# Attention heads of an mLSTM and mixture-of-experts layer taken in pairs, their score products alternating between the two halves of the array's rows

## What is computed

```
xn   = layernorm(x)                       # queries
ig,fg= gates from [xn, ctx, ctx]          # 8 + 8 rows per token
cs   = cumsum(log_sigmoid(fg))
logD[s,t] = cs[s] - cs[t] + ig[t]   for t <= s, else -inf
Dmat = exp(logD - max_t logD)
C    = (xn_h @ ctx_h.T / 8) * Dmat        # 256 x 256, lower triangle, per head
h    = C / (max(|sum C|, exp(-max logD)) + 1e-6) @ ctx_h
x    = x + tanh(g0) * layernorm(h) * ln_scale
```

## Time and profile before

| | |
|---|---|
| runs | 1310.32, 1306.76, 1304.9 us; median 1306.76 |
| span of the profiled execution | 1302.3 us, first to last instruction; its own total time is not listed apart |
| PE busy | 1098.4 us, 84% |
| PEld | 910.9 us, 70% |
| DVE | 827.1 us, 64% |
| ACT | 371.4 us, 29% |
| POOL | 491.8 us, 38% |

### The profile page before, as it was taken

The page is one execution under the profiler, slowest core; times in us unless marked ns, Lnnn a source line. Parts: engine busy times, 40 slices in busy tenths (PEclk is TensorE's granted clock), DMA queues, the critical chain, the costliest instruction groups (busy, mean ns, idle before and its releaser), DMA issues.

```text
span 1302.3 us, 24291 instructions
## 1 busy us (share of the span) xinstructions
PE 1098.4 (84%) x6611; PEld 910.9 (70%) x6612; DVE 827.1 (64%) x2212; ACT 371.4 (29%) x820; POOL 491.8 (38%) x368
## 2 busy tenths in 40 slices
PE   2289999999999999999999765999999999999000
PEld 1167888878788887788788664788888888887000
DVE  3756878888788788788877644544444444444455
ACT  1133233424333333343333102223233232232000
POOL 3600222222222222222212335356656566700775
PEclk9666999999999999999999778999999999999555
DMA  5000001110111011001000244555464645321787
GB/s 205 32 33 33 33 34 66 57 42 32 65 57 41 33 65 65 17 32 49 33 1 34 82 172 156 175 181 176 158 205 149 209 151 187 128 98 64 239 283 260
DMA packets 57869, 134.53 MB, mean 103 GB/s; under 512 B 7088, under 2 KB 7088, under 8 KB 57808
## 3 DMA queue, kind: packets, MB, share of 16 engines
q0 software_dynamic: 17472, 59.78, 14.0%
q1 hardware_dynamic: 26128, 48.51, 11.2%
q10 hardware_dynamic: 14208, 25.57, 5.5%
HBM read 83.23 MB, written 50.59 MB: 103 GB/s over the span
## 4 chain that ended last, share of the span: by engine, by line
PE 72%; DVE 12%; issue 7%; DMA 5%; ACT 2%; POOL 0%; DVEq 0%; ACTq 0%; POOLq 0%
PE bank L1137 18%; PE bank L1001 10%; PE bank L1155 9%; PE bank L1012 7%; PE bank L937 5%; PE bank L913 5%; DMA area<-routed_y,y_at 4%; PE bank L879 3%; PE bank L1125 3%; PE bank L942 2%; PE bank L954 2%; PE bank L939 2%; PE bank L955 2%; PE bank L957 2%; PE bank L1146 1%
## 5 line engine op out<-in xcount | busy, mean ns | idle before, releaser
L1137 PE MATMUL bank<-w_ring,x2nT 128*128 x960 | 246.0, 405 | 8.6 <-DVE w_ring L1597 8.6
L1137 PEld LDWEIGHTS bank<-w_ring,x2nT 128*128 128x128 f32 x960 | 175.3, 189 | 48.9 <-issue 10.0
L1001 PE MATMUL bank<-x2nT,w_ring 128*128 128x256 f32 x1536 | 200.2, 288 | 7.8 <-DVE sh_act L1434 7.8
L1001 PEld LDWEIGHTS bank<-x2nT,w_ring 128*128 128x128 f32 x1536 | 190.2, 194 | 9.2 <-DVE sh_act L1434 5.4
L501 POOL DMA_INDIRECT routed_x<-x2n,slot_u x64 | 67.5, 1054 | 192.9 <-DVE slot_u L1424 178.3
L1288 DVE SCALAR_TENSOR_TENSOR area<-bank,area 128x384 f32<-128x384 f32 x128 | 71.4, 557 | 96.7 <-ACT area L712 61.4
L1155 PE MATMUL bank<-w_ring,sh_actT 128*128 x480 | 125.2, 396 | 2.1 <-DVE sh_actT L1616 2.1
L1603 DVE SCALAR_TENSOR_TENSOR ctxT<-ctxT,bank 128x256 f32<-128x256 f32 x80 | 33.7, 421 | 142.7 <-ACT ctxT L826 142.7
L710 ACT ACTIVATE area<-bank,key_log 128x256 f32<-128x256 f32 x128 | 60.7, 474 | 212.1 <-PE bank L944 176.2
L522 POOL TENSOR_TENSOR sh_actT<-sh_act,sh_actT 128x256 fp32r<-128x256 f32 x64 | 54.5, 852 | 167.9 <-ACT sh_actT L727 167.8
L618 POOL TENSOR_TENSOR w_ring<-area,one 128x3072 fp32r<-128x3072 f32 x14 | 74.3, 5304 | 114.4 <-PE bank L1155 114.4
(11 more groups left out here) (203 smaller groups left out, 2059.0 us busy)
## 6 DMA issues: line engine op xcount, KB each, us to landing
x2n<-routed_x SPq DMA_DIRECT2D x80, 256.0 KB, 2.8
routed_y<-cs_in ACTq DMA_DIRECT2D x80, 256.0 KB, 2.1
base_out<-in_x_dram SPq DMA_DIRECT2D x16, 512.0 KB, 4.4
cs_in<-in_ctx_dram SPq DMA_DIRECT2D x16, 512.0 KB, 3.7
area<-n_L_ffn_expert_gate_dram POOLq DMA_DIRECT2D x16, 512.0 KB, 4.1
area<-in_L_ffn_expert_up_dram POOLq DMA_DIRECT2D x16, 512.0 KB, 4.9
area<-n_L_ffn_expert_down_dram POOLq DMA_DIRECT2D x16, 512.0 KB, 6.9
out_dram<-area SPq DMA_DIRECT2D x32, 256.0 KB, 4.2
```

The costliest lines, as they stand in the source:

```text
L1001: last = mm(GU[m][:, at:at + S], w[:, w_part, c, m * P:(m + 1) * P], x2nT[:, x_part, c, :], start=(c + p == 0), stop=(c == DC - 1 and p == 2))
L1137: last = mm(bank[2 + t.par][:, :], xtT[:, x_part, t.par, c * P:(c + 1) * P], w_gu[:, bass.ds(slot, 1), w_part, c, :].rearrange("p a i -> p ...
```

## The change

The eight heads are taken two at a time. PE's `head` becomes `pair(b, q)`, which makes the scores of heads `2q` and `2q + 1` with the products of the two alternating, then spreads both maxima. `c_made` and `decay_made` of both heads of the pair before must be in. The number and size of all products stay. The `step` lists of ACT, PE and DVE are put in an order that follows; POOL's and SP's stay as they are.

```diff
-            def head(b, h):
-                k = h % 2
-                rows = slice(DH * (h % 2), DH * (h % 2) + DH)
-                c = h // 2
+            def pair(b, q):
                 pe.wait_ge(xnT_made.sem, xnT_made.upto(b.n))
                 pe.wait_ge(ctxT_made.sem, ctxT_made.upto(b.n))
                 pe.wait_ge(row_step.sem, row_step.upto(b.n))
-                pe.wait_ge(c_made.sem, c_made.upto(b.n, h - 1))
-                pe.wait_ge(decay_made.sem, decay_made.upto(b.n, h - 1))
-                mm(QK[k][:, 0:S], ctxT[rows, b.par, c, 0:P], xnT[rows, b.par, c, 0:S],
-                   start=True, stop=True)
-                mm(QK[k][:, S:TRI], ctxT[rows, b.par, c, P:S], xnT[rows, b.par, c, P:S],
-                   start=True, stop=True).then_inc(qk_made.sem, 1)
-                for at, n in ((0, S), (S, P)):
-                    mm(MB[k][:, at:at + n], head_sel[0:96, h, :], max_parts[0:96, b.par, S - n:S],
-                       start=True, stop=False)
-                    last = mm(MB[k][:, at:at + P], identb[:, :], mask_b[:, :], start=False, stop=True)
-                last.then_inc(max_spread.sem, 1)
+                pe.wait_ge(c_made.sem, c_made.upto(b.n, 2 * q))
+                pe.wait_ge(decay_made.sem, decay_made.upto(b.n, 2 * q))
+                for at, frm, n in ((0, 0, S), (S, P, P)):
+                    for k in range(2):
+                        half = slice(DH * k, DH * (k + 1))
+                        last = mm(QK[k][:, at:at + n], ctxT[half, b.par, q, frm:frm + P], xnT[half, b.par, q, S - n:S],
+                                  start=True, stop=True)
+                        if at:
+                            last.then_inc(qk_made.sem, 1)
+                for k in range(2):
+                    for at, n in ((0, S), (S, P)):
+                        mm(MB[k][:, at:at + n], head_sel[0:96, 2 * q + k, :], max_parts[0:96, b.par, S - n:S],
+                           start=True, stop=False)
+                        last = mm(MB[k][:, at:at + P], identb[:, :], mask_b[:, :], start=False, stop=True)
+                    last.then_inc(max_spread.sem, 1)
```

The rest of the diff moves calls within the three `step` lists. The lists of a full step, before (-) and after (+), with the calls in one line:

```
- ACT head 0, keep(H,1), shared(H,2), head 1, turn_ctx 0, keep(H,2), shared(H,3), head 2, turn_ctx 1,
      keep(H,3), head 3, turn_x 0, head 4, turn_x 1, top(H), head 5, turn(G,0), head 6, turn(G,1),
      head 7, log_gates(F), shared(G,0), keep(G,0), shared(G,1), columns(F)
+ ACT head 0, 1, keep(H,1), shared(H,2), turn_ctx 0, head 2, 3, keep(H,2), shared(H,3), turn_ctx 1,
      keep(H,3), head 4, 5, turn_x 0, turn_x 1, top(H), head 6, 7, turn(G,0), log_gates(F), turn(G,1),
      shared(G,0), keep(G,0), shared(G,1), columns(F)

- PE  head 0, shared(H,2), head 1, pv 0, turn_ctx 0, shared(H,3), head 2, pv 1, turn_ctx 1,
      shared_down(H,0), head 3, turn_x 0, pv 2, head 4, turn_x 1, pv 3, shared_down(H,1), gates_pe(F),
      head 5, turn(G,0), pv 4, head 6, turn(G,1), rank(H), pv 5, head 7, router(G), shared(G,0),
      logits(G), pv 6, shared(G,1), columns(F), pv 7
+ PE  pair 0, shared(H,2), pv 0, pv 1, turn_ctx 0, pair 1, shared(H,3), pv 2, pv 3, turn_ctx 1, pair 2,
      shared_down(H,0), turn_x 0, pv 4, pv 5, turn_x 1, pair 3, shared_down(H,1), gates_pe(F), pv 6,
      pv 7, turn(G,0), rank(H), turn(G,1), router(G), shared(G,0), logits(G), shared(G,1), columns(F)

- DVE head 0, h_stats(G), shared(H,2), head 1, center(G), stats(N), shared(H,3), head 2,
      norm_front(F,0), x2_add(G), out_pair 0, shared_down(H,0), head 3, norm_front(F,1), x2_stats(G),
      head 4, out_pair 1, post_norm(G), top(H), shared_down(H,1), head 5, turn(G,0), read_gates(F),
      head 6, turn(G,1), rank(H), head 7, out_pair 2, router(G), rows(F), shared(G,0), keep_logits(G),
      shared(G,1), columns(F), out_pair 3
+ DVE head 0, 1, h_stats(G), shared(H,2), center(G), x2_add(G), out_pair 0, head 2, 3, stats(N),
      shared(H,3), x2_stats(G), out_pair 1, norm_front(F,0), head 4, 5, post_norm(G),
      shared_down(H,0), norm_front(F,1), out_pair 2, top(H), head 6, 7, shared_down(H,1),
      read_gates(F), turn(G,0), rank(H), out_pair 3, turn(G,1), router(G), rows(F), shared(G,0),
      keep_logits(G), shared(G,1), columns(F)
```

More of the change, by code:

```diff
@@ L739, in step @@
                     head(A, 0)
+                    head(A, 1)
                 if rest:
@@ L766, in step @@
                 if attend:
-                    head(A, 5)
+                    head(A, 6)
+                    head(A, 7)
                 if route:
                     turn(G, 0)
-                if attend:
-                    head(A, 6)
+                if front:
+                    log_gates(F)
                 if route:
                     turn(G, 1)
[L774 to L777, removed]
                 if route:
@@ L1024, in step @@
                 if attend:
-                    head(A, 0)
+                    pair(A, 0)
                 if rest:
@@ L1057, in step @@
                 if attend:
-                    head(A, 5)
+                    pv(A, 6)
+                    pv(A, 7)
                 if route:
                     turn(G, 0, front)
-                if attend:
-                    pv(A, 4)
-                    head(A, 6)
+                if rest and route:
+                    rank(H, front, attend)
                 if route:
                     turn(G, 1, front)
-                if rest and route:
-                    rank(H, front, attend)
-                if attend:
-                    pv(A, 5)
-                    head(A, 7)
-                if route:
                     router(G, front)
@@ L1479, in step @@
                     shared(H, 3)
-                if attend:
-                    head(A, 2)
-                if front:
-                    norm_front(F, 0)
-                if route:
-                    x2_add(G)
-                if attend:
-                    out_pair(A, 0)
-                if rest:
-                    shared_down(H, 0)
-                if attend:
-                    head(A, 3)
-                if front:
-                    norm_front(F, 1)
                 if route:
@@ L1496, in step @@
                 if attend:
+                    out_pair(A, 1)
+                if front:
+                    norm_front(F, 0)
+                if attend:
                     head(A, 4)
-                    out_pair(A, 1)
+                    head(A, 5)
                 if route:
                     post_norm(G)
+                if rest:
+                    shared_down(H, 0)
+                if front:
+                    norm_front(F, 1)
+                if attend:
+                    out_pair(A, 2)
                 if rest and route:
                     top(H)
+                if attend:
+                    head(A, 6)
+                    head(A, 7)
                 if rest:
                     shared_down(H, 1)
-                if attend:
-                    head(A, 5)
+                if front:
+                    read_gates(F)
                 if route:
                     turn(G, 0)
-                if front:
-                    read_gates(F)
-                if attend:
-                    head(A, 6)
-                if route:
-                    turn(G, 1)
                 if rest and route:
@@ L1517, in step @@
                 if attend:
-                    head(A, 7)
-                    out_pair(A, 2)
+                    out_pair(A, 3)
                 if route:
+                    turn(G, 1)
                     router(G)
```

47 lines of the change are left out of this document (22 added, 25 removed).

## The result

The changed kernel took 1339.25 us (median of 4 runs, 1337.45 to 1341.46) against 1308.54 for the kernel before on the same chip: a ratio of 1.0239 with a 95% interval of 1.0210 to 1.0268. It is 2.4% slower; forecast were 1357 us and a range of 1318 to 1382. The profiled span is 1335.9 us, 33.6 more than before.

What follows compares the result with a forecast made beforehand. PE was taken to bound, with DVE's late results in program order deciding. Thirteen steps of waits (27 us) and clock (23 us) add 50 us to 1306.8, giving 1357 us; range 1318 to 1382.

Steps and rivals of the forecast that it cites:

- waits, but a clock that holds: Rival: same waits, but idle stretches too short to lower the clock; 1334 us, chance 0.30.
- Score products: PE's scores and spreading for two heads: different row groups run concurrently; a pair was counted at 1.8 us.
- Front half: Start of the first pair to xn's second turn: PE ready at 19.5 us, xn at 21.1; PE waits 1.6 us.
- After the branch: The step following DVE's loop branch, every second one, has 1.4 us more of waiting.
- turn(G,1): Second turn of x2n on PE: only rank lies between the turns, so PE waits 1.5 us for DVE.
- router: PE's router waits 2.3 us for DVE's remainder of turn(G,1), held to 36.2 us by DVE's and ACT's queues alike.
- Tail: From router to next pair: router 1.51, two shared blocks 5.9, small turns with waits 0.7 us; next pair at 44.3.
- A full step's waits: Waits in each of steps 2 to 14: 2.1 us more on average, 13 x 2.1 = 27 us.
- The ends: Steps 0, 1 and 15, which lack some parts: put at nothing, 3 us either way.
- Clock: Clock falls just ahead of the router in most steps, returns within router and shared(G,0): 1.8 us a step, 23 in all.
- PE goes on to bound: Rival: both waits, 1.6 and 3.8 us, mostly wrong, so a step gets shorter; 1275 us, chance of faster 0.10.

Runs made afterwards that it cites:

- e4: Changed kernel plus 9 unneeded products ahead of turn(G,1) and 15 ahead of the router, in steps that have all parts; 1319.62 us, ratio 1.0107 to the kernel before.
- e5: Changed kernel with a pair's score products not alternating: all four passes of the even head, then four of the odd; 1339.79 us, ratio 1.0232.
- e9: e6 with both heads of a pair reading rows 0 to 63, so the odd heads' own scores are left out; 1311.34 us, ratio 1.0013.
- e1: Changed kernel with log_gates(F) put behind turn(G,1) again on ACT; 1336.0 us, ratio 1.0250 to the kernel before.
- e2: Changed kernel with out_pair(A,3) put behind turn(G,1) on DVE; 1338.06 us, ratio 1.0256 to the kernel before.
- e6: Changed kernel with PE's turn(G,0) behind the fourth pair, turn(G,1) behind shared_down(H,1), both ahead of the gates, ACT and DVE following; 1285.45 us, ratio 0.9817.
- e10: e6 with DVE's `top` cut in two, one-hots and weights moved behind turn(G,1); 1277.64 us, ratio 0.9754 to the kernel before.
- e3: Changed kernel with both log_gates (ACT) and out_pair(A,3) (DVE) put behind turn(G,1); 1335.24 us, ratio 1.0228 to the kernel before.
- e7: Changed kernel with DVE's norm_front(F,0) and norm_front(F,1) put ahead of x2_stats, post_norm and shared_down(H,0) as inputs allow; 1339.06 us, ratio 1.0231.
- e11: e10 with e7's order on DVE (norm_front(F,0) ahead of out_pair 1, x2_stats behind heads 4 and 5); 1302.89 us, ratio 0.9950.
- e12: e10 with each pair's PE work head by head, scores and spread products of the even head, then the odd; 1316.27 us, ratio 1.0064.
- e8: Changed kernel with the reorderings of e6 and e7 together; 1331.23 us, ratio 1.0173 to the kernel before.

## Why the prediction was right, and where its sizes were off

Slower was right, and by the mechanism forecast: waits of PE for DVE around the two turns of x2n, and a clock that falls because of them. The sum was too high by 19 us: 50 us forecast, 31 (2.4%) measured. By its time alone the result lies in the range of the rival "waits, but a clock that holds"; the granted clock in the windows and e4 exclude that rival. The waits and the clock were both put too high, and the first and last steps, which were put at nothing, gave time back. Of the 19 us some 7 are the clock's, 5 those of the ends and 4 those of the full steps' waits, by the traces; the rest lies between traces and medians.

**Score products: 1.8 us a pair, measured 1.41.** The first score product starts 0.86 us before the first spread product, and the next block 1.41 us after it. The forecast let neighbouring passes overlap only where they lie side by side in the order of issue, five slots. They fall into four, each the size of one head's pass, though each product's two passes were issued together; so a pair's scores cost what one head's do (0.86 against 0.85). The rule of the Trainium skill, "TensorE: Matmul & The Clock Gate", Part 3, that products in different row groups run concurrently, is borne out by e5 and e9. The starts lay 6 to 7 ns apart, and 14 in e5, not the some 4 of the forecast's rule.

**Front half: 1.6 us, measured 2.08.** The waits are 0.75, 0.48 and 0.85 us, 0.5 more, as PE's own work up to there was 0.5 shorter than forecast: what PE gained, it waited. xn's turn starts 21.1 us into the step (413.09 to 434.16), as forecast. Here the forecast's statement that the waits swallow most of the scores' price was right.

**After the branch: 1.4 us more, measured 0.9.** Laps alternate between 45.7 and 46.6 us (before: 42.2 and 43.6 to 43.7).

**turn(G,1): 1.5 us, measured 1.36; router: 2.3, measured 2.29.** That both ACT's logarithm and DVE's rank and out_pair hold it, and that undoing one alone would not help, e1 and e2 show; they end within 0.02 us of each other.

**Tail: 8.1 us, measured 9.95** (449.07 to 459.02), of which the clock is 1.5: 0.4 more than forecast, in short waits ahead of the next pair.

**A full step's waits: 2.1 us, and 27 in all; measured 1.8 and 24.** From the first router to the 14th, thirteen steps, e4 takes 23.6 us more than the kernel before.

**The ends: nothing, 3 us either way; measured -5.** From the 14th router on DVE has less to do (30 us of work in the next step, where a full one has 34 to 35), and the shorter pairs show as a gain: the next two steps are 3.0 and 2.7 us shorter in e4 than before, against 0.6 us lost up to the first router. In the changed kernel 4.1 us are gained at the end and 0.8 at the start. Besides the five slots above, this is where a step of the forecast failed, and not only a size. With them e4's trace is 18.5 us longer up to the experts; by the medians 14 are left.

**Clock: 1.8 us a step and 23 in all; measured 1.2 and 16 from the traces, 17 from the medians.** This is the term that was furthest off. In the step shown, the router's products take 2.70 us start to start for 1.51, 1.2 more, and shared(G,0) 3.21 for 2.9, 0.3 more: the clock is full again by 453, 1.2 us into it. The forecast had it slow for longer, from rows behind another wait.

**The rival "PE goes on to bound".** It was put at 1275 us, should both waits be mostly wrong. They were there. e6 and e10 take the ones at the turns away, by order alone, and reach 1285 and 1278. That this is near the rival's 1275 us is in part luck: its waits for xn stayed (0.50 and 0.85 us in e10), and the ends gave time back.

## What to carry to other kernels

A change that makes the bounding engine's work shorter also takes away what lay between a result and its use. Before taking it, list for each hand-over (here PE, ACT, DVE, PE: 2.1 us) what is left between producer and consumer, and put a block of independent work of that length there; here the same 3.5 us saved a step were a loss of 2.4% in one order and a gain of 2.5% in another. When two queues hold the same result, mend both, and look at which wait the clock falls after; shortening a wait may do no more than move the point where it falls (e3). And an engine that comes early isn't a gain by itself: e7 and e11 made PE wait less in one place and more in a worse one.

## What the runs showed of the hardware

- Products in the two halves of the array's rows ran side by side even when all four passes of one were issued ahead of the other (e5: starts 14 ns apart; 0.87 us for eight passes). In each of e5's 64 pairs the four passes of 256 columns ran ahead of the four of 128. In one half the same eight took 1.48 us (e9).
- Twenty-four products of no use a step, in waits of 1.36 and 2.29 us, made the kernel 17 us faster (e4). Without them the granted clock went from 1.00 to 0.50 (1.2 GHz), behind the second wait in the step shown and within it in the step before.
- The length of a wait alone doesn't tell whether the clock falls. The waits of 0.75, 0.48 and 0.85 us left it at full speed in the step shown; in another step of the changed kernel it fell behind three of nearly the same length (0.73, 0.50 and 0.85, at 247.6 us), and in the step after the one shown behind a single one of 1.28 us. Behind the wait of 1.36 us it was still full in the step shown and had fallen in e3 and e7. What set these apart stays open.
- Losing the overlap (2.5 us of PE's work a step in e9, 3.5 in e12) cost 18 and 17 us up to the first router, where the clock was at 0.50 for most of the time, against 0.45 and 1.7 us in a later lap.
- DVE's first instruction of x2n (128x512) took 1.23 us beside a copy on POOL of 1.03 us (e7, e8, e11), and 0.53 us without one (e10).
